# Layer 1 attention of an eight-layer kernel: the softmax's row sums from VectorE's reduction of the probabilities, or from ScalarE's accumulators

## The chip, the cores and the metric

The kernel runs on one core of one Trainium2 chip, as one program. The metric is its device time in microseconds (us), as the median of several executions.

## The reference, cut to what matters

The whole program is four pairs of a gated cross attention and a gated feed-forward layer, L0 to L3, on x of 16 batches x 128 positions x 256 features, with a context of the same shape. The part that the change touches is the attention of L1. For each batch b and each of 8 groups g it computes, with two query heads on x itself and two on the context:

```python
def _ln(x, w, b):
    mu = jnp.mean(x, axis=-1, keepdims=True)
    var = jnp.mean(jnp.square(x - mu), axis=-1, keepdims=True)
    return (x - mu) * jax.lax.rsqrt(var + EPS) * w + b
def _fp8_linear_pertensor(x, wq, w_scale, in_scale):
    xq = _div_clamp_fp8(x, in_scale)
    return jnp.einsum('bsi,oi->bso', xq * in_scale, wq) * w_scale
def _gqa(q, k, v):
    scale = 1.0 / np.sqrt(q.shape[-1])
    scores = jnp.einsum('bsghd,btgd->bghst', q, k) * scale
    p = jax.nn.softmax(scores, axis=-1)
    return jnp.einsum('bghst,btgd->bsghd', p, v)
```

Queries and keys go through `_ln` per head before `_gqa`; the heads' outputs are rounded to fp8 and projected back, and the result is added to x. The softmax needs, for every row of 128 scores, the maximum, the exponentials and their sum.

## The kernel before

A stage of the program is a list of instructions per engine; a stage starts when the signals of the one before have come. `l1_attention` first prepares weights and then runs one software pipeline over N = 128 units n = 8 b + g (16 batches x 8 groups). Everything stays on chip but the context, which is loaded once per batch. Each engine walks the same **steps** s and does in each step the work of several units, written out by hand in `tensor`, `scalar`, `vector` and `gpsimd` (lines 808 to 1040). An engine takes its instructions in that order, and a wait holds all that stands behind it. I count steps by s modulo 8 ("step 4" is s = 4, 12, 20, ...). In step s:

- TensorE: `project` of unit s-9 (L742, L745), `score` of s-12 (L754; waits for the exponentials of the unit before, s-13, since there is one bank of scores), `values` of s-14 (L763), `out_project` of s-15 (L775), `turn_heads` of s-11 (L787; waits for the norm of s-11), `turn_probs` of s-13 (L795; waits for GpSimd's scaled probabilities). In step 3 also `turn_x` (L803), the transposes of the next batch's x, which wait for ScalarE's `put_heads`.
- ScalarE: `exponent` of s-13 (L829: four activations of 128x128, one per head, each with the negated row maxima as its bias; an accumulator gives each row's sum), then the copies `put_probs` (L837) and `raw` (L846, L847), then `put_heads` of s-11 (L855, L857). In step 3 it ends with `scale_inputs` (L865, and eight activations L872) for the next batch.
- VectorE: in step 7 the sum into x (L962, L965); `quantise_out` of s-15 (L927, L899 to L906), its six instructions alternating with six `bn_stats` of s-10 (L914); in steps 4 to 7 and 0 one of the five parts of `quantise_x` for the next batch (L899, L901, L903, L905, L906 on 1024 columns; the first waits for `scale_inputs`, the last, which writes l1_xq, for the projections of the current batch); in step 3 the normalised x of the next batch (L975); then the reciprocal of the row sums of s-13 (L980), which waits for `exponent`; the norm of s-11 (six L985), which waits for GpSimd's `statistics`; and the negated maxima of s-12 (L993), which wait for `score` and for which the next step's `exponent` waits.
- GpSimd: the probabilities of s-13 times the inverse sums (L1034, waits for L980), then `statistics` of s-10, a chain of small operations on 128x6 that ends with L1026.

Names: PR is l1_pr (two buffers of 128x4x128, in fp32), rowsum is l1_rowsum (128x4 twice), pscore the bank of scores. `dve_own` is a semaphore that VectorE raises for itself where one of its instructions reads what another wrote.

Batches come once in eight steps. The five parts of `quantise_x` fall behind a `scale_inputs` whose step-3 chain runs through TensorE and ScalarE, for the batches 1 to 15 of the pipeline; the first of these (s = 12 to 16) lies in the ramp, where several of the other functions have no unit yet, and 14 follow with all of it.

Of the kernel before, what the change touches and what calls it, by code (L numbers as in the profile page):

```python
# [12 lines left out]
ALU = mybir.AluOpType  # L13
ACT = mybir.ActivationFunctionType
AXX = mybir.AxisListType.X
# [67 lines left out]
def build(nc, A, out):  # L83
    ctx = ExitStack()
    with ctx:
# [3 lines left out]
        def sb(scope, name, shape, dt=F32):  # L89
            return scope.enter_context(nc.sbuf_tensor(name, shape, dt))  # L90
# [5 lines left out]
        def begin(e, ends):  # L96
            for sem, value in ends:
                e.wait_ge(sem, value)

        dve_own = Own(ctx.enter_context(nc.semaphore("dve_own")))  # L100
# [488 lines left out]
        def l1_attention(ends, loaded, W, WX, scratch):  # L589
# [36 lines left out]
            negmax = sb(scratch, "l1_negmax", [P, 2, 4])  # L626
            rowsum = sb(scratch, "l1_rowsum", [P, 2, 4])
            PR = sb(scratch, "l1_pr", [P, 2, 4, P])
# [195 lines left out]
            def exponent(e, n):  # L824
                e.wait_ge(*s_max(n + 1))
                if n >= 2:
                    e.wait_ge(*s_ptr(n - 1))
                for h in range(4):
                    r = e.activation(PR[:, n % 2, h, :], pscore[:, h * P:(h + 1) * P], ACT.Exp,  # L829
                                     bias=negmax[:, n % 2, h:h + 1], accum_out=rowsum[:, n % 2, h:h + 1])  # L830
                r.then_inc(s_exp.sem, 1)

            def put_probs(e, n):
# [42 lines left out]
            def scalar(e):  # L876
                begin(e, ends)
                for s in range(G + N + 8):
                    if 0 <= s - 13 < N:
                        exponent(e, s - 13)  # L880
                    if s % G == 0 and 0 <= s // G - 1 < B:
                        b = s // G - 1
                        e.wait_ge(*s_ctx(b + 1))
                        if b >= 1:
                            e.wait_ge(*s_proj(G * b))
                        e.copy(tok(CX[:, :, :]), tok(CN[:, :, :])).then_inc(s_cx.sem, 1)
                    if 0 <= s - 14 < N:
                        put_probs(e, s - 14)
                    if 0 <= s - 9 < N:
                        raw(e, s - 9)  # L890
                    if 0 <= s - 11 < N:
                        put_heads(e, s - 11)
                    if s % G == 3 and s // G < B:
                        scale_inputs(e, s // G)
# [23 lines left out]
            def quantise_out(e, n):  # L918

                own = None  # L920
                for part in range(6):
                    if 0 <= n < N:
                        if part == 0:
                            e.wait_ge(*s_pv(n + 1))
                            if n >= 1:
                                e.wait_ge(*s_cat(n))
                            e.tensor_tensor(YO[:, :].rearrange("p (h t) -> p h t", h=4),  # L927
                                            pout[:, :].rearrange("p (h t) -> p h t", h=4),
                                            bc(smooth[:, n % G, :], 2, P), ALU.mult).then_inc(s_smooth.sem, 1)
                        else:  # L930
                            e.wait_ge(*(s_smooth(n + 1) if part == 1 else own))
                            if part == 5 and n >= 2:
                                e.wait_ge(*s_outp(n - 1))
                            r = round_fp8(e, part - 1, YO[:, :], EO[:, :], TO[:, :], tok(CAT[:, n % 2, :, :]))
                            if part == 5:
                                r.then_inc(s_cat.sem, 1)
                            else:
                                dve_own.did(r)
                                own = dve_own.all()
                    count(e, n + 5, part)  # L940
# [3 lines left out]
            def quantise_x(e, b, part):  # L944
                e.wait_ge(*(quantised[b] if part else s_affine(b + 1)))
                if part == 4 and b >= 1:
                    e.wait_ge(*s_proj(G * b))
                r = round_fp8(e, part, YQ[:, :], EQ[:, :], TQ[:, :], XQ[:, :, :, :].rearrange("p n k t -> p (n k t)"))
                if part == 4:
                    r.then_inc(s_xq.sem, 1)  # L950
                else:
                    dve_own.did(r)
                    quantised[b] = dve_own.all()

            def vector(e):
                begin(e, ends)
                for s in range(G + N + 9):
                    n = s - 16
                    if 0 <= n < N and n % G == G - 1:
                        b = n // G  # L960
                        e.wait_ge(*s_outp(n + 1))
                        e.scalar_tensor_tensor(X[:, b, :], pacc[:, 0:D], coef[:, 0:1], X[:, b, :],  # L962
                                               ALU.mult, ALU.add).then_inc(s_xadd.sem, 1)
                        e.wait_ge(*s_xadd(b + 1))
                        e.bn_stats(stats[:, b, :], X[:, b, :]).then_inc(bn.sem, 1)  # L965
                    quantise_out(e, s - 15)
                    if s % G >= 4 and s // G < B:
                        quantise_x(e, s // G, s % G - 4)
                    if s % G == 0 and 1 <= s // G <= B:
                        quantise_x(e, s // G - 1, 4)  # L970
                    if s % G == 3 and s // G < B:
                        b = s // G
                        if b >= 1:
                            e.wait_ge(*s_xtr(b))
                        e.tensor_scalar(xn[:, :], X[:, b, :], mean[:, b:b + 1], rstd[:, b:b + 1],  # L975
                                        ALU.subtract, ALU.mult).then_inc(s_xn.sem, 1)
                    n = s - 13
                    if 0 <= n < N:
                        e.wait_ge(*s_exp(n + 1))
                        e.reciprocal(rowsum[:, n % 2, :], rowsum[:, n % 2, :]).then_inc(s_inv.sem, 1)  # L980
                    n = s - 11
                    if 0 <= n < N:
                        e.wait_ge(*s_rstd(n + 1))
                        for m in range(6):
                            r = e.tensor_scalar(RAW[:, n % 4, m, :], RAW[:, n % 4, m, :], tiny[:, n % 2, 0, m:m + 1],  # L985
                                                tiny[:, n % 2, 6, m:m + 1], ALU.subtract, ALU.mult)
                        r.then_inc(s_norm.sem, 1)
                    n = s - 12
                    if 0 <= n < N:
                        e.wait_ge(*s_score(n + 1))  # L990
                        if n >= 2:
                            e.wait_ge(*s_exp(n - 1))
                        e.tensor_reduce(negmax[:, n % 2, :], pscore[:, :].rearrange("p (h t) -> p h t", h=4),  # L993
                                        AXX, ALU.max, negate=True).then_inc(s_max.sem, 1)
# [33 lines left out]
            def gpsimd(e):  # L1028
                begin(e, ends)
                for s in range(G + N + 8):  # L1030
# [5 lines left out]
                    if 0 <= s - 10 < N:  # L1036
                        statistics(e, s - 10)

            stage(sync=sync, tensor=tensor, scalar=scalar, vector=vector, gpsimd=gpsimd)
            return [bn(B), s_outp(N), s_pte(N), s_prob(N), s_cx(B), s_rstd(N)]  # L1040

# [1004 lines left out]
```

## Time and profile before

| | |
|---|---|
| median of 3 runs | 2855.9 us (2855.89 to 2860.24) |
| the profiled execution's own time | 2857.04 us |
| its span in the profile | 2855.2 us |
| busy, share of the span | PE 86%, PE's weight loads 72%, DVE 71%, ACT 45%, POOL 41% |
| granted TensorE clock, mean | 0.931 |

PE is TensorE, DVE VectorE, ACT ScalarE, POOL GpSimd. The attention of L1 takes some 1000 us of the span, from about 640 to 1645 us. A busy engine of a whole program says little about one stage, so the views of the stage are read for the change: the busy time in a stretch, the instructions in order of time on one engine, and the waits.

### The profile page before, as it was taken

How to read it: one execution, taken by the hardware profiler on the slowest of the kernel's cores; microseconds unless marked ns; L12 is line 12 of the kernel's file. 1: busy time of each engine (PE TensorE's matmuls, PEld its weight loads, DVE VectorE, ACT ScalarE, POOL GpSimd, SP SyncE). 2: the span in 40 equal slices, each digit the busy share in tenths (PEclk: the TensorE clock that was granted, in tenths of full speed). 3: DMA queues.
4: the chain of work that ended last, by engine and by line, in shares of the span. 5: the costliest groups of instructions: out<-in, count | busy, mean ns of one | idle time of the engine just before them, and what ended most of it. 6: DMA issues, size and time to landing. Idle time of an engine off the chain costs nothing. (4 is left out here: it accounts for less than half of the span.)

```text
span 2855.2 us, 51398 instructions
## 1 busy us (share of the span) xinstructions
PE 2451.8 (86%) x17090; PEld 2057.1 (72%) x17090; DVE 2037.1 (71%) x5105; ACT 1296.4 (45%) x3941; POOL 1179.1 (41%) x2615
## 2 busy tenths in 40 slices
PE   5758999939999999999999869999699997466997
PEld 2346777728888888888888858888588886234775
DVE  7964555558888888888888847777554554895776
ACT  0013333236666666666666623333144443344663
POOL 4401000037777777777777711111143443122112
PEclk9768999969999999999999969999799999676998
DMA  2030000010000000000000030000100000001000
GB/s 73 17 133 24 16 16 8 1 63 3 3 3 5 3 3 3 3 3 3 3 5 1 1 106 23 23 23 12 52 7 9 7 5 1 0 1 53 21 24 31
DMA packets 29155, 56.72 MB, mean 20 GB/s; under 512 B 4846, under 2 KB 22574, under 8 KB 27422
## 3 DMA queue, kind: packets, MB, share of 16 engines
q1 hardware_dynamic: 28894, 53.43, 5.7%
q8 instruction: 140, 2.29, 0.3%
q14 instruction: 121, 0.99, 0.1%
HBM read 51.33 MB, written 2.10 MB: 19 GB/s over the span
## 5 line engine op out<-in xcount | busy, mean ns | idle before, releaser
L434 PE MATMUL bank<-m_xr,m_wgr 128*88 128x512 f32 (+1 forms) x1824 | 442.3, 395 | 17.4 <-POOL m_wgr L494 17.4
L434 PEld LDWEIGHTS bank<-m_xr,m_wgr 128*88 128x88 f32 (+1 forms) x1824 | 307.3, 172 | 116.9 <-issue 19.5
L742 PE MATMUL bank<-l_w,l_xq 128*128 128x128 f32 (+1 forms) x2048 | 358.5, 328 | 9.9 <-DVE l_xq L906 7.1
L742 PEld LDWEIGHTS bank<-l_w,l_xq 128*128 128x128 f32 x2048 | 300.4, 192 | 31.1 <-DVE l_xq L906 7.5
L985 DVE TENSOR_SCALAR xn_T<-xn_T,l_tiny 128x128 f32<-128x128 f32 x768 | 297.2, 453 | 8.4 <-POOL l_tiny L1026 8.4
L494 POOL TENSOR_TENSOR m_wgr<-m_wg,m_wgr 128x512 fp32r<-128x512 f32 (+1 forms) x28 | 40.3, 1440 | 585.5 <-ACT m_wgr L472 585.5
L855 ACT ACTIVATE l_qt<-bank,l_head_b,l_head_w 128x256 f32<-128x256 f32 x256 | 144.6, 565 | 287.5 <-PE bank L787 287.5
L447 PEld LDWEIGHTS bank<-m_wdr,m_hbr 88*128 88x128 f32 (+1 forms) x1824 | 233.1, 192 | 26.9 <-DVE m_hbr L549 18.0
L447 PE MATMUL bank<-m_wdr,m_hbr 88*128 88x256 f32 (+1 forms) x1824 | 239.5, 285 | 10.1 <-DVE m_hbr L549 10.0
L582 DVE SCALAR_TENSOR_TENSOR x_resident<-bank,m_cg,x_resident 128x256 f32<-128x256 f32 x448 | 185.9, 478 | 85.4 <-PE bank L447 79.4
L484 ACT ACTIVATE m_sg<-bank 88x512 f32<-88x512 f32 (+1 forms) x152 | 90.8, 597 | 323.0 <-PE bank L434 323.0
L914 DVE BATCH_NORM_STATS2 l_st<-xn_T 128x6 f32<-128x128 f32 x768 | 214.3, 282 | 12.7 <-ACT l_v L847 12.5
L572 DVE TENSOR_TENSOR m_ht<-m_sg,bank 88x512 f32<-88x512 f32 (+1 forms) x152 | 104.3, 686 | 146.8 <-ACT m_sg L484 146.5
L1034 POOL TENSOR_TENSOR l_pr<-l_pr,l_rowsum 128x512 f32<-128x512 f32 x128 | 134.3, 1050 | 156.9 <-DVE l_rowsum L980 156.9
L829 ACT ACTIVATE l_pr<-bank,l_negmax 128x128 f32<-128x128 f32 x512 | 182.4, 385 | 1.6 <-DVE l_negmax L993 1.6
L1016 POOL TENSOR_TENSOR l_tiny<-l_tiny,l_consts 128x6 f32<-128x6 f32 x128 | 177.6, 1387 | 10.0
L775 PE MATMUL bank<-l_wp,l_cat 128*128 128x256 f32 x1024 | 167.1, 306 | 2.0 <-DVE l_cat L906 2.0
L754 PEld LDWEIGHTS bank<-l_qt 128*128 128x128 f32 x1024 | 133.8, 192 | 45.4 <-issue 39.7
L754 PE MATMUL bank<-l_qt 128*128 128x128 f32 x1024 | 137.2, 277 | 33.5 <-ACT l_pr L829 33.5
L1322 POOL TENSOR_TENSOR l_pr<-l_pr,l_rowsum 128x512 f32<-128x512 f32 x64 | 66.6, 1041 | 206.1 <-DVE l_rowsum L1289 206.1
L846 ACT COPY xn_T<-bank 128x384 f32<-128x384 f32 x256 | 125.7, 491 | 46.8 <-PE bank L745 46.8
L775 PEld LDWEIGHTS bank<-l_wp,l_cat 128*128 128x128 f32 x1024 | 140.4, 190 | 9.0 <-DVE l_cat L906 2.4
(272 smaller groups left out, 5715.2 us busy)
## 6 DMA issues: line engine op xcount, KB each, us to landing
l_w<-in_l_w SPq DMA_DIRECT2D x1, 6144.0 KB, 17.3
m_wg<-in_m_gu SPq DMA_DIRECT2D x18, 256.0 KB, 2.6
m_wg<-in_m_gu SPq DMA_DIRECT2D x10, 352.0 KB, 2.9
l2f_w<-in_l_w SPq DMA_DIRECT2D x3, 1024.0 KB, 7.5
m_wd<-in_m_down SPq DMA_DIRECT2D x18, 128.0 KB
x_resident<-in_x SPq DMA_DIRECT2D x4, 512.0 KB, 5.6
l_ctxT<-in_ctxT SPq DMA_DIRECT2D x1, 2048.0 KB, 7.1
l_toep<-in_l_toep SPq DMA_DIRECT2D x16, 128.0 KB, 2.0
```

Source lines behind the costliest of these rows:

```text
L434: r = e.matmul(banks[2 * (q % 2) + half][0:M, :], WGR[:, u % 2, a, k, sub, half, :], XR[:, b, k, cols], start=k == 0 and n == 0, stop=k == ...
L447: r = e.matmul(banks[4 + 2 * (n % 2) + s // 2][:, (s % 2) * D:(s % 2 + 1) * D], HBR[0:M, n % 2, a, sub, s * P:(s + 1) * P], WDR[0:M, u % 2 ...
L582: r = e.scalar_tensor_tensor(X[:, b, :], banks[4 + 2 * (n % 2) + s // 2][:, (s % 2) * D:(s % 2 + 1) * D], CG[:, u, b:b + 1], X[:, b, :], A ...
L742: e.matmul(bank[:, to:to + width], XQ[:, v, k, :], W[:, k, g, at:at + width], start=k == 0, stop=k == KT - 1)
L754: r = e.matmul(pscore[:, h * P:(h + 1) * P], QT[:, n % 2, x + h % 2, :], QT[:, n % 2, x + 2, :], start=True, stop=True)
L775: r = e.matmul(pacc[:, 0:D], CAT[:, n % 2, h, :], WP[:, part, head, :], start=g == 0 and h == 0 and part == 0, stop=g == G - 1 and h == 3 ...
L829: r = e.activation(PR[:, n % 2, h, :], pscore[:, h * P:(h + 1) * P], ACT.Exp, bias=negmax[:, n % 2, h:h + 1], accum_out=rowsum[:, n % 2, h ...
L855: e.activation(tok(QT[:, n % 2, 3 * x:3 * x + 2, :]), ps[:, 0:2 * P], ACT.Identity, bias=head_b[:, 2 * x:2 * x + 1], scale=head_w[:, 2 * x ...
L914: r = e.bn_stats(st[:, n % 2, m, :], RAW[:, n % 4, m, :])
L985: r = e.tensor_scalar(RAW[:, n % 4, m, :], RAW[:, n % 4, m, :], tiny[:, n % 2, 0, m:m + 1], tiny[:, n % 2, 6, m:m + 1], ALU.subtract, ALU. ...
L1016: pool_own.did(e.tensor_tensor(r0, var, minus_half, ALU.pow))
L1034: e.tensor_tensor(PR[:, n % 2, :, :], PR[:, n % 2, :, :], bc(rowsum[:, n % 2, :], 2, P), ALU.mult).then_inc(s_prob.sem, 1)
```

## The change

The four activations of `exponent` no longer have an accumulator. VectorE adds up the probabilities of the unit with one `tensor_reduce` of 128x512 to 128x4, behind the wait for the exponentials, waits for it by its own semaphore, and takes the reciprocal as before. The numbers that reach GpSimd are the same sums of the same exponentials.

```diff
                 for h in range(4):
                     r = e.activation(PR[:, n % 2, h, :], pscore[:, h * P:(h + 1) * P], ACT.Exp,
-                                     bias=negmax[:, n % 2, h:h + 1], accum_out=rowsum[:, n % 2, h:h + 1])
+                                     bias=negmax[:, n % 2, h:h + 1])
                 r.then_inc(s_exp.sem, 1)
...
                     n = s - 13
                     if 0 <= n < N:
                         e.wait_ge(*s_exp(n + 1))
+                        dve_own.did(e.tensor_reduce(rowsum[:, n % 2, :], PR[:, n % 2, :, :], AXX, ALU.add))
+                        e.wait_ge(*dve_own.all())
                         e.reciprocal(rowsum[:, n % 2, :], rowsum[:, n % 2, :]).then_inc(s_inv.sem, 1)
```

## Rows read from the trace of the kernel before

**Rows 1.** Busy time by engine in a stretch (count of instructions), granted clock, DMA share, GB/s.
```profile
640.00:1640.00 1000.00, 933.40 (x6293) 864.27 (x6292) 858.18 (x2630) 660.50 (x2295) 769.39 (x2127) 1.00 0.01 3
```

**Rows 2.** TensorE in order of time: start, us, line, operation, [idle before, released by].
```profile
1017.63 1.13 PE L754 MATMUL bank<-l_qt 128*128 128x128 f32 x8 [1.69 <-ACT l_pr L829]
...
1020.42 0.82 PE L787 MATMUL bank<-ident,xn_T 128*128 128x128 f32 x6
...
1042.41 0.88 PE L787 MATMUL bank<-ident,xn_T 128*128 128x128 f32 x6
...
1050.92 0.88 PE L787 MATMUL bank<-ident,xn_T 128*128 128x128 f32 x6 [0.60 <-DVE xn_T L985]
...
1058.27 0.82 PE L787 MATMUL bank<-ident,xn_T 128*128 128x128 f32 x6
...
1065.56 0.82 PE L787 MATMUL bank<-ident,xn_T 128*128 128x128 f32 x6
```

**Rows 3.** VectorE in order of time, steps 4 to 2 of the same batch.
```profile
1016.13 0.43 DVE L899 TENSOR_SCALAR l_yq<-l_yq 128x1024 bf16<-128x1024 bf16 x1 [3.76 <-ACT l_yq L872]
1017.52 0.18 DVE L980 RECIPROCAL l_rowsum<-l_rowsum 128x4 f32<-128x4 f32 x1 [0.96 <-ACT l_pr L829]
1017.61 2.33 DVE L985 TENSOR_SCALAR xn_T<-xn_T,l_tiny 128x128 f32<-128x128 f32 x6
...
1023.77 0.40 DVE L901 TENSOR_SCALAR l_eq<-l_yq 128x1024 uint16<-128x1024 uint16 x1
...
1024.82 2.36 DVE L985 TENSOR_SCALAR xn_T<-xn_T,l_tiny 128x128 f32<-128x128 f32 x6 [0.21 <-POOL l_tiny L1026]
...
1031.81 2.32 DVE L985 TENSOR_SCALAR xn_T<-xn_T,l_tiny 128x128 f32<-128x128 f32 x6
...
1035.19 0.48 DVE L962 SCALAR_TENSOR_TENSOR x_resident<-bank,l_coef,x_resident 128x256 f32<-128x256 f32 x1 [0.46 <-PE bank L775]
1035.71 0.43 DVE L965 BATCH_NORM_STATS2 ln_stats<-x_resident 128x6 f32<-128x256 f32 x1
...
1039.35 0.68 DVE L905 TENSOR_TENSOR l_tq<-l_yq,l_eq 128x1024 bf16<-128x1024 bf16 x1
1039.94 0.17 DVE L980 RECIPROCAL l_rowsum<-l_rowsum 128x4 f32<-128x4 f32 x1
...
1047.32 1.23 DVE L906 TENSOR_TENSOR l_xq<-l_tq,l_eq 128x1024 f32<-128x1024 bf16 x1 [1.05 <-PE bank L745]
...
1048.55 2.32 DVE L985 TENSOR_SCALAR xn_T<-xn_T,l_tiny 128x128 f32<-128x128 f32 x6
...
1055.50 2.36 DVE L985 TENSOR_SCALAR xn_T<-xn_T,l_tiny 128x128 f32<-128x128 f32 x6 [0.33 <-POOL l_tiny L1026]
...
1062.27 0.18 DVE L980 RECIPROCAL l_rowsum<-l_rowsum 128x4 f32<-128x4 f32 x1 [0.51 <-ACT l_pr L829]
```

**Rows 4.** ScalarE in order of time, the exponentials of step 4.
```profile
1016.00 0.36 ACT L829 ACTIVATE l_pr<-bank,l_negmax 128x128 f32<-128x128 f32 x1
1016.25 0.20 ACT L829 ACTIVATION_READ_ACCUMULATOR l_pr<-bank,l_negmax 128x1 f32 x1
...
1017.28 0.21 ACT L829 ACTIVATION_READ_ACCUMULATOR l_pr<-bank,l_negmax 128x1 f32 x1
```

**Rows 5.** ScalarE in order of time, exponentials of L3's attention, which have no accumulator.
```profile
2700.16 1.61 ACT L1709 ACTIVATE l_pr<-bank,l_negmax 128x256 f32<-128x256 f32 x4
2701.59 1.14 ACT L1720 COPY l_pt<-bank 128x512 f32<-128x512 f32 x2
```

**Rows 6.** VectorE's groups by form: count, busy us, mean ns, idle before.
```profile
L993 DVE TENSOR_REDUCE l_negmax<-bank 128x4 f32<-128x512 f32 x128 | 86.8, 678 | 1.1 <-PE bank L754 1.1
...
L322 DVE TENSOR_REDUCE l_sums<-l_z 128x64 f32<-128x512 f32 x64 | 66.9, 1066 | 0.0
...
L1513 DVE TENSOR_REDUCE l2f_sc<-l2f_xr 128x1 f32<-128x256 f32 x16 | 6.7, 420 | 0.6
```

**Rows 7.** Waits in the stage: who waited for whom, total us, times, longest.
```profile
PE bank L754 <- ACT l_pr L829: 33.5, 18, 2.9
```

## The prediction

> **What bounds the kernel now.** I read the stage's busy times first, then TensorE in order of time over one batch, then VectorE over the same batch, then ScalarE at the one place where TensorE waits for it. From 640 to 1640 us TensorE is busy 93% of the time and VectorE 86%, at the full granted clock of 1.00, its 2.4 GHz level [rows 1]: two engines are close to the bound, so the question is where the second becomes the first. An ordinary step lasts 1065.56 - 1058.27 = 7.29 us, without a wait on TensorE [rows 2]; there VectorE sits idle 0.51 us before its reciprocal, behind a wait for GpSimd of 0.33 [rows 3]. Such steps are TensorE's. But in three places of each batch another wait ends last:
>
> - step 4: ScalarE's exponentials start late, behind the eight activations of `scale_inputs`, and TensorE's `score` waits 1.69 us for them [rows 2]; VectorE waits 3.76 us for `scale_inputs` and 0.96 us for the exponentials [rows 3];
> - step 7: `turn_heads` starts at 1042.41, just when the norm that began at 1040.03 is through; VectorE had no idle time before that step's reciprocal;
> - step 0: TensorE idles 0.60 us before `turn_heads` for the norm (L985) [rows 2], which stands behind the last part of `quantise_x`, itself held 1.05 us by the projections [rows 3].
>
> So from step 4 to step 0 VectorE's own sequence is already the bound in two places. Work added to it there lengthens the batch, and work added in steps 1 to 3 goes into its idle time.
>
> **What the change removes.** Per unit, four accumulator reads. The activations of a unit start 0.34 us apart and each read follows its activation by 0.25 us [rows 4]: (1017.28 - 1016.25) / 3 = 0.34. Without reads I take the next activation to start 0.25 behind the one before. Activations of L3 bear that out from the other side: four of 256 columns without accumulators take 2701.59 - 2700.16 = 1.43 us of issue, 0.36 each, for twice the columns [rows 5]. The last exponential of step 4 then ends at 1016.00 + 3 x 0.25 + 0.36 = 1017.11, against 1017.28 + 0.21 = 1017.49 now: 0.38 us earlier in every step. Bounds: none of it is saved but the last read, 0.1 us (the activations keep their 0.34), or all of 0.38; I take 0.38, since two different rows give it. By the Trainium skill (ScalarE: Activation LUTs, What ACT_TABLE_LOAD costs) back-to-back activations overlap by only about 93 ns; by that estimate the exponentials of 128 columns would follow each other by some 0.29 us and end about 0.13 later than I take. The row of step 4 shows an overlap of 0.11 (0.36 - 0.25) up to the read, so it disagrees a little, and the sum would rise by about 0.13 us per batch, 2 us in all.
>
> In ordinary steps these 0.38 us are worth nothing: ScalarE is idle behind them anyway. In step 4 `score` starts 0.38 earlier. In the drain of the pipeline, where `score` waits for the exponentials too (18 waits in all, the longest 2.9 us, some four of them in the drain [rows 7]), I credit 4 x 0.38 = 1.5 us.
>
> **What it adds.** One reduction of 128x512 per unit on VectorE, 128 in all. The reduction of the maxima has the same shape, but from PSUM, and takes 0.678 us; one from SBUF of 256 columns takes 0.420, and L322, also 512 columns from SBUF but adding elements that lie 8 apart, 1.066 [rows 6]. The new one reads neighbouring elements, as L993 and L1513 do: 0.68. Then the reciprocal has to wait for it. Independent VectorE instructions overlap by 0.09 (L905 of 0.68 us, the next 0.59 after its start), while one that waits for its forerunner starts 0.04 behind its end (L962 of 0.48 us, L965 0.52 after its start) [rows 3]. So the reduction costs 0.68 + 0.04 = **0.72 us** of VectorE's sequence before the reciprocal. Bounds: 0.59 (nothing for the wait, the overlap of a free instruction) and 1.11 (L322's duration). The Trainium skill (VectorE: DVE Perf Modes, The DRAIN you can't avoid) says that a semaphore between VectorE instructions costs nothing extra. By that rule the reciprocal would start about 0.59 behind the reduction and the total would come out near +14 us; the pair L962 and L965 speaks against it, as the dependent one pays 0.52 for a duration of 0.48.
>
> What stands behind the added wait: on VectorE the norm (L985) and the maxima (L993); on GpSimd L1034 and `statistics`; on TensorE `turn_heads` and, with much time to spare, `turn_probs`. In a step where VectorE is idle before the reciprocal, that comes 0.72 - 0.38 = 0.34 us later; `turn_heads` is not touched: in step 2 the norm ends at 1062.27 + 0.09 + 2.33 = 1064.69 and `turn_heads` starts at 1065.56 [rows 2, 3], so of 0.87 us of slack 0.53 are left.
>
> **The walk through a batch**, all times 10xx.xx of rows 3 with the new cost put in:
>
> - step 4: exponentials end 17.11, reduction at 17.15 (as the reciprocal now starts 0.03 behind them), reciprocal 17.87, norm 17.96 (now 17.61).
> - step 5: 6.16 us (1023.77 - 1017.61) to L901, 24.12; reduction 0.31 later, when its 0.40 are issued, 24.43; norm at 24.43 + 0.72 + 0.09 = 25.24 (now 24.82, when it waited 0.21 for GpSimd). GpSimd's chain from one norm to the next is 7.21 here (24.82 - 17.61): 25.17, just hidden.
> - step 6: by the same spacings, 25.24 + 6.16 + 0.31 + 0.81 = 32.52 (now 31.81).
> - step 7: L962 now starts after an idle 0.46 for TensorE, 2.9 us behind the norm without it; it starts at 35.42 (now 35.19), L905 4.16 later at 39.58, reduction 40.17, norm at 40.98 (now 40.03): **+0.95**. TensorE had no slack here: `turn_heads` moves from 42.41 to 43.36.
> - step 0: the projections, and with them L906 (47.32), move by the 0.95; behind it the reduction adds its 0.72 in full, since there was no idle time before the reciprocal: norm at 48.55 + 0.95 + 0.72 = 50.22, **+1.67**. `turn_heads` waited for the norm already and moves as much.
> - step 1: GpSimd's chain, 6.95 from norm to norm (55.50 - 48.55), gives 57.17; VectorE's own, 6.26 us from the norm to the end of the work before the reciprocal (1062.27 - 0.51 - 55.50 in the next step), less an overlap of 0.09, and 0.81, gives 57.20; again +1.67, and no more. Steps 2 and 3: TensorE's, unchanged; the norm is 0.35 later than due and has its 0.5 us.
>
> The earlier `score` of step 4 is worth nothing: `turn_heads` would be ready at 1020.04 in place of 1020.42 [rows 2], but waits for the norm, 17.96 + 2.33 + 0.05 = 20.34.
>
> **Sum.** 14 full batches x 1.67 = 23.4 us; the ramp's batch, with less on VectorE, between 0 and 1.67, taken at 0.7; the drain -1.5, and +0.3 for the last unit's later reciprocal: **+22.9 us**. The profiled execution took 2857.04 us for a span of 2855.2; it would take 2879.9. Against the median of 2855.9, 1.1 below that execution, it is 2878.8; I say 2879. A measurement of this kernel can tell about 0.2%, 5.7 us, from no change.
>
> **Rivals.**
>
> 1. *The reduction is hidden, no change.* This needs VectorE to add the numbers at twice the rate of L993. The walk counts the reduction four times up to +0.95 and five times up to +1.67, so the step 0 delay vanishes at 0.72 - 1.67 / 5 = 0.39 us. From 256 to 512 columns a reduction grows by 0.678 - 0.420 = 0.258; at twice the rate 512 columns cost what 256 do now, 0.42 + 0.04 = 0.46, 0.35 us per batch, +4 us: 2860. For it: nothing but that other VectorE operations have such rates; against it: all three reductions in rows 6 take 1 ns per column or more (0.258 us for the 256 further columns). 8%.
> 2. *Faster.* The 0.38 us that the exponentials end earlier decide step 4, and VectorE takes the reduction into its waits. The place is step 0: below 0.39 us per reduction the batch gets shorter, by 0.39 less the cost. With a cost as small as the reciprocal's 0.09 that would be 0.3 x 14 + 1.5 = 5.7 us, 2851. Against it: no reduction in the trace is under 0.39 at this size. 3%.
> 3. *VectorE bounds every step.* With L322's 1.11 the five counts add 5 x 0.39 = 1.95 to the 1.67, and an ordinary step of VectorE, 6.3 us from one reciprocal to the place of the next, grows to 7.4, over TensorE's 7.29; with step 3's extra instruction some 0.5 us more per batch. 4.1 x 14 = 58, about 2914. For it: the buffer is in SBUF, as L322's. Against it: L1513. 5%.
> 4. *ScalarE saves nothing* since activations keep 0.34: the exponentials of step 4 end 0.28 later than I take, 14 x 0.28 = 4 us more and no gain in the drain: 2884. 6%, still slower.
>
> The forecast's own mechanism, with the bounds of its terms, has the remaining 78%. Its own ends: 0.59 per reduction gives 1.67 - 5 x 0.13 = 1.02 per batch and +14 (2870); 0.85, if the reduction is held up by GpSimd or the wait costs more than L965's, gives +9 more (2888). The range reaches to most of the no-change case below and past rival 4 above, for stalls of TensorE that the walk doesn't see: 2863 to 2896. Faster 3% is rival 2; within 0.2% 9% is rival 1 and 1% of the forecast's low end; the rest, 88%, is slower.
>
> **What the changed profile would show.** L829's activations about 0.25 us apart and no accumulator reads; 128 new reductions at L980's place of 0.68 us, the reciprocal 0.72 behind their start; in step 0 the norm 1.67 us later within the batch, TensorE's idle before `turn_heads` grown from 0.60 to about 1.3, and in step 7 a new one of about 0.8; ordinary steps still 7.29. I am wrong if the reduction takes under 0.5 or over 0.9 us, if the ordinary steps grow, or if GpSimd's chain rather than VectorE's ends last in step 5 or 6.

## The result, and the profile after

The changed kernel takes **2879.9 us** (median of 4 runs, 2879.7 to 2885.4) against 2857.5 for the kernel before in the same comparison: a ratio of 1.0081 (95% interval 1.0068 to 1.0093). The forecast was slower, 2879 us, with a range of 2863 to 2896. The profiled execution took 2879.81 us for a span of 2878.0, 22.8 us over the span of before. Two lines are new, so the reduction is L980, the reciprocal L982, GpSimd's scaling L1036, the norm L987, the maxima L995.

Busy time of the stretch that [rows 1] shows for before:

```profile
640.00:1640.00 1000.00, 922.15 (x6187) 851.11 (x6185) 914.96 (x2702) 601.70 (x1752) 772.38 (x2095) 1.00 0.01 3
```

TensorE is down from 93.3% to 92.2%, VectorE up from 86% to 91%, ScalarE down from 66% to 60%, at the same clock. VectorE in order of time over one batch after the change, steps 4 to 2, which answers to [rows 3]:

```profile
1090.42 0.43 DVE L899 TENSOR_SCALAR l_yq<-l_yq 128x1024 bf16<-128x1024 bf16 x1 [3.39 <-ACT l_yq L872]
1091.43 0.69 DVE L980 TENSOR_REDUCE l_rowsum<-l_pr 128x4 f32<-128x512 f32 x1 [0.58 <-ACT l_pr L829]
1092.15 0.18 DVE L982 RECIPROCAL l_rowsum<-l_rowsum 128x4 f32<-128x4 f32 x1
1092.25 2.32 DVE L987 TENSOR_SCALAR xn_T<-xn_T,l_tiny 128x128 f32<-128x128 f32 x6
...
1098.72 0.67 DVE L980 TENSOR_REDUCE l_rowsum<-l_pr 128x4 f32<-128x512 f32 x1
...
1099.53 2.32 DVE L987 TENSOR_SCALAR xn_T<-xn_T,l_tiny 128x128 f32<-128x128 f32 x6
...
1106.81 2.32 DVE L987 TENSOR_SCALAR xn_T<-xn_T,l_tiny 128x128 f32<-128x128 f32 x6
1109.05 0.68 DVE L995 TENSOR_REDUCE l_negmax<-bank 128x4 f32<-128x512 f32 x1
1109.65 0.47 DVE L962 SCALAR_TENSOR_TENSOR x_resident<-bank,l_coef,x_resident 128x256 f32<-128x256 f32 x1
...
1115.19 2.32 DVE L987 TENSOR_SCALAR xn_T<-xn_T,l_tiny 128x128 f32<-128x128 f32 x6
...
1122.48 1.22 DVE L906 TENSOR_TENSOR l_xq<-l_tq,l_eq 128x1024 f32<-128x1024 bf16 x1 [1.05 <-PE bank L745]
1123.62 0.68 DVE L980 TENSOR_REDUCE l_rowsum<-l_pr 128x4 f32<-128x512 f32 x1
1124.33 0.18 DVE L982 RECIPROCAL l_rowsum<-l_rowsum 128x4 f32<-128x4 f32 x1
1124.42 2.33 DVE L987 TENSOR_SCALAR xn_T<-xn_T,l_tiny 128x128 f32<-128x128 f32 x6
...
1131.38 2.35 DVE L987 TENSOR_SCALAR xn_T<-xn_T,l_tiny 128x128 f32<-128x128 f32 x6
```

Between the wait for the exponentials of step 4 (0.58) and that for the projections in step 0 (1.05) the view shows no idle time of VectorE. The norms start 7.28, 7.28, 8.38 and 9.23 us apart; before it was 7.21, 6.99, 8.22 and 8.52. TensorE, which answers to [rows 2], in the same batch:

```profile
1091.54 1.13 PE L754 MATMUL bank<-l_qt 128*128 128x128 f32 x8 [1.30 <-ACT l_pr L829]
1094.62 0.88 PE L787 MATMUL bank<-ident,xn_T 128*128 128x128 f32 x6
...
1117.57 0.88 PE L787 MATMUL bank<-ident,xn_T 128*128 128x128 f32 x6 [0.87 <-DVE xn_T L987]
...
1126.81 0.87 PE L787 MATMUL bank<-ident,xn_T 128*128 128x128 f32 x6 [1.33 <-DVE xn_T L987]
...
1134.15 0.82 PE L787 MATMUL bank<-ident,xn_T 128*128 128x128 f32 x6
```

`score` in step 4 waits 1.30 in place of 1.69; step 7 has a wait of 0.87 that was not there; that of step 0 has grown from 0.60 to 1.33; the ordinary step behind it takes 7.34 us from one `turn_heads` to the next, the one after that 7.29. ScalarE in step 4 of that batch, and VectorE's two reductions by form, which answer to [rows 4] and [rows 6]:

```profile
1090.30 1.10 ACT L829 ACTIVATE l_pr<-bank,l_negmax 128x128 f32<-128x128 f32 x4
```

```profile
L980 DVE TENSOR_REDUCE l_rowsum<-l_pr 128x4 f32<-128x512 f32 x128 | 86.7, 678 | 18.1 <-ACT l_pr L829 17.9
L995 DVE TENSOR_REDUCE l_negmax<-bank 128x4 f32<-128x512 f32 x128 | 86.6, 676 | 0.9 <-PE bank L754 0.9
```

Four exponentials take 1.10 us from the first start to the last end (I took 3 x 0.25 + 0.36 = 1.11), and the reduction 0.678 (I took 0.68).

**Where the 22.8 us lie.** I read the start of the first `project` instruction (L742) of a unit in both traces. The first are those of unit 8, the second those of unit 120, before:

```profile
671.03 2.79 PE L742 MATMUL bank<-l_w,l_xq 128*128 128x256 f32 x16
...
1560.26 2.79 PE L742 MATMUL bank<-l_w,l_xq 128*128 128x256 f32 x16
```

and after:

```profile
672.22 2.79 PE L742 MATMUL bank<-l_w,l_xq 128*128 128x256 f32 x16
...
1583.51 2.79 PE L742 MATMUL bank<-l_w,l_xq 128*128 128x256 f32 x16
```

Fourteen batches take 889.2 us before, 63.52 each, and 911.3 after, 65.09 each: **+22.1 us**, 1.58 per batch. Unit 0 starts at 614.63 before and 613.43 after, 1.20 earlier (that is ahead of the changed part, and differs as much between executions of other kernels below); counted from there, the ramp up to unit 8 adds 2.39. From the last unit's `project` on, the drain gives back 0.9. -1.2 + 2.4 + 22.1 + 0.3 (the seven steps from unit 120 to 127) - 0.9 = 22.7.

### The profile page after: what moved, and what is told of

Its sections match the earlier page's. It is cut to its first block and busy times, and to the rows that moved or that the text cites. A ratio compares the mean times of both kernels' runs of the same rounds, so it can differ in the third digit from the quotient of the medians.

```text
span 2878.0 us, 51014 instructions
## 1 busy us (share of the span) xinstructions
PE 2455.1 (85%) x17090; PEld 2059.8 (72%) x17090; DVE 2115.0 (73%) x5233; ACT 1248.7 (43%) x3429; POOL 1193.9 (41%) x2615
## 5 line engine op out<-in xcount | busy, mean ns | idle before, releaser
L742 PE MATMUL bank<-l_w,l_xq 128*128 128x128 f32 (+1 forms) x2048 | 360.2, 329 | 9.9 <-DVE l_xq L906 7.1
L742 PEld LDWEIGHTS bank<-l_w,l_xq 128*128 128x128 f32 x2048 | 301.8, 193 | 31.4 <-DVE l_xq L906 7.5
L987 DVE TENSOR_SCALAR xn_T<-xn_T,l_tiny 128x128 f32<-128x128 f32 x768 | 296.2, 452 | 0.0
L1036 POOL TENSOR_TENSOR l_pr<-l_pr,l_rowsum 128x512 f32<-128x512 f32 x128 | 135.2, 1056 | 166.0 <-DVE l_rowsum L982 166.0
L829 ACT ACTIVATE l_pr<-bank,l_negmax 128x128 f32<-128x128 f32 x512 | 147.1, 387 | 1.6 <-DVE l_negmax L995 1.6
L549 DVE TENSOR_TENSOR m_hbr<-m_ht,m_hbr 88x512 fp32r<-88x512 f32 (+1 forms) x152 | 125.6, 826 | 28.9 <-ACT m_hbr L488 28.9
```

The lines of the kernel that those rows point to most:

```text
L742: e.matmul(bank[:, to:to + width], XQ[:, v, k, :], W[:, k, g, at:at + width], start=k == 0, stop=k == KT - 1)
L1036: e.tensor_tensor(PR[:, n % 2, :, :], PR[:, n % 2, :, :], bc(rowsum[:, n % 2, :], 2, P), ALU.mult).then_inc(s_prob.sem, 1)
```

## The experiments

The theory was that of the forecast: VectorE's order from the exponentials of step 4 to the norm of step 0 sets the length of a batch, the reduction costs it 0.72 us at a time, and what ScalarE saves counts once, 0.38 us in step 4. The rivals: that the saving is worth nothing; that VectorE's total work counts, wherever it stands; that the waits of TensorE have other causes. "Per batch" below is read as above, from unit 8 to unit 120 over 14; the kernel before had medians of 2857.0 to 2858.8 us in these comparisons.

| kernel | median us | ratio to before, 95% | per batch us |
|---|---|---|---|
| before | 2857.0 to 2858.8 | | 63.52 |
| changed | 2879.9 | 1.0068 to 1.0093 | 65.09 |
| e1, accumulators and reduction | 2890.1 | 1.0097 to 1.0128 | 65.48 |
| e2, neither | 2850.7 | 0.9963 to 0.9985 | 63.13 |
| e3, two reductions | 2952.7 | 1.0319 to 1.0347 | 69.74 |
| e4, sums first in step 0 | 2871.4 | 1.0033 to 1.0058 | 64.39 |
| e5, change in steps 1 to 3 | 2857.1 | 0.9992 to 1.0011 | 63.48 |
| e6, change in steps 4 to 0 | 2884.5 | 1.0080 to 1.0107 | 65.10 |
| e7, norm ahead, accumulators | 2845.0 | 0.9939 to 0.9964 | 62.67 |
| e8, norm ahead, changed | 2850.7 | 0.9964 to 0.9982 | 63.15 |
| e9, change in step 4 | 2859.6 | 0.9998 to 1.0016 | 63.47 |
| e10, norm ahead, change in step 4 | 2839.2 | 0.9923 to 0.9948 | 62.32 |
| e11, as e7 | 2842.1 | 0.9939 to 0.9966 | 62.67 |
| e12, GpSimd's scaling cut | 2852.0 | 0.9964 to 0.9982 | 63.11 |

**e1: accumulators and reduction.**

```diff
-                                     bias=negmax[:, n % 2, h:h + 1])
+                                     bias=negmax[:, n % 2, h:h + 1], accum_out=rowsum2[:, n % 2, h:h + 1])
```

> The changed kernel with the accumulators back, written to a tile that nobody reads; the reduction stays. Theory (VectorE's sequence from the exponentials of step 4 to the norm of step 0 sets the batch; the reduction costs it five times, the reads' removal gives back 0.38 us once, in step 4): the exponentials of step 4 end 0.38 us later and the whole chain with them, 15 x 0.38 and 4 x 0.38 in the drain, about +7 us on the changed kernel, 2887 us. Rival (taking the reads away was worth nothing, and what was measured is the reduction alone): as the changed kernel, 2880.

2890.1 us, +0.39 us per batch on the changed kernel, and `score` waits 1.68 again. The median is 3 us over the forecast, the profiled execution is at 2887.9. Of the batch only step 4 is longer, from one `project` to the next 9.56 us in place of 9.18: the reads are worth 0.38 there, where VectorE's chain starts behind them, and nothing in the other steps.

**e2: neither.** The row sums are left out.

```diff
-                        dve_own.did(e.tensor_reduce(rowsum[:, n % 2, :], PR[:, n % 2, :, :], AXX, ALU.add))
-                        e.wait_ge(*dve_own.all())
-                        e.reciprocal(rowsum[:, n % 2, :], rowsum[:, n % 2, :]).then_inc(s_inv.sem, 1)
+                        e.reciprocal(rowsum[:, n % 2, :], ones4[:, :]).then_inc(s_inv.sem, 1)
```

> The kernel before without the accumulators and without any sum: the reciprocal is taken of a constant tile, so the probabilities are scaled by a constant and the row sums are left out. Theory: 0.38 us per batch in step 4 and four times in the drain, 7 us under the kernel before, 2850 us. Rival (the earlier score is lost again at the next wait, by step 7 at the latest): same as the kernel before, 2857.

2850.7 us, 0.39 per batch under the kernel before. So the change has two parts that add up: the saving, -0.39, and the reduction, 65.09 - 63.13 = +1.96 per batch; with the accumulators kept (e1 against the kernel before) it is 65.48 - 63.52 = 1.96 too.

**e3: a second reduction** into a tile that nobody reads, ahead of the first.

```diff
+                        dve_own.did(e.tensor_reduce(rowsum2[:, n % 2, :], PR[:, n % 2, :, :], AXX, ALU.add))
                         dve_own.did(e.tensor_reduce(rowsum[:, n % 2, :], PR[:, n % 2, :, :], AXX, ALU.add))
```

> The changed kernel with a second reduction of the same probabilities into a tile that nobody reads, ahead of the first, so VectorE has 0.59 us more per unit. Theory: five times 0.59 = 2.95 us per batch in steps 4 to 0, and now VectorE's ordinary step (6.26 + 0.59 + 0.81 - 0.09 = 7.57) is over TensorE's 7.29, so steps 1 to 3 add 0.28, 0.28 and 0.59 less the 0.5 of slack: about 3.6 us per batch, 14 x 3.6 = 50, about 2930 us (2920 to 2945), and idle time of TensorE before turn_heads in every step. Rival (each reduction costs what the first did, 23 us, with ordinary steps still TensorE's): 2903.

2952.7 us, beyond the 2945 that I had allowed: 4.65 per batch on the changed kernel in place of 3.6. The linear rival is out, and so is my sum. TensorE in step 0 and its granted clock around it (the second fence: stretch, length, busy, clock, DMA share, GB/s):

```profile
1090.10 0.88 PE L788 MATMUL bank<-ident,xn_T 128*128 128x128 f32 x6 [1.92 <-DVE xn_T L989]
...
1091.45 4.24 PE L743 MATMUL bank<-l_w,l_xq 128*128 128x256 f32 x16
```

```profile
1088.00:1090.00 2.00, 0.19 (x2) 1.00 0.00 0
1090.00:1092.00 2.00, 1.90 (x12) 0.76 0.04 8
1092.00:1094.00 2.00, 2.00 (x8) 0.50 0.00 0
1094.00:1096.00 2.00, 2.00 (x13) 0.89 0.01 4
```

With one reduction TensorE idled 1.33 us there at most; now it idles 1.92, and in this batch its clock falls from the 2.4 to the 1.2 GHz level behind that. The 16 instructions take 4.24 us in place of 2.79. The wait alone does not decide it: of the fourteen waits of 1.85 to 1.92 us in step 0 of the full batches six are followed by such a fall and eight are not, and two more falls come behind waits of 1.47 us for `put_heads` in step 3. The four batches that no fall touches take 69.13 or 69.14 us, 4.04 over the changed kernel, and the average is 69.74, so the falls are 8.6 of the 15 us that my sum missed. The other 6 lie in step 3, which grew by 0.57 us where I had put 0.09: with VectorE the bound in steps 1 and 2 already, the slack that I subtracted was gone, and TensorE waits 0.36 us for the norm there. The norms are 7.88 and 7.87 apart in steps 5 and 6, the 0.59 more that the theory gave.

**e4: sums first in step 0**, reduction and reciprocal moved ahead of the last part of `quantise_x`. `inverse` holds the wait for the exponentials, the reduction, its wait and the reciprocal.

```diff
+                    early = s % G == 0
+                    if early:
+                        inverse(s - 13)
...
                     if s % G == 0 and 1 <= s // G <= B:
                         quantise_x(e, s // G - 1, 4)
```

> The changed kernel, but in step 0 VectorE takes reduction and reciprocal ahead of the last part of quantise_x, into the 1.06 us that it idles there for the projections. Theory (in step 0 the reduction stands in full between the projections' end and the norm that TensorE waits for): the norm of step 0 starts 0.81 us earlier, 14 x 0.81 = 11 us under the changed kernel, 2869 us; TensorE's idle before turn_heads in step 0 falls from 1.32 to about 0.5. Rival (TensorE's wait there is set by the last part of quantise_x or by GpSimd's chain, not by the reduction): 2880.

2871.4 us; TensorE's wait in step 0 falls from 1.33 to 0.60, and a batch is shorter by 0.70 of the 0.81 us. Here a second thing shows, VectorE and GpSimd in order of time:

```profile
1055.02 1.94 DVE L906 TENSOR_TENSOR l_xq<-l_tq,l_eq 128x1024 f32<-128x1024 bf16 x1 [0.26 <-PE bank L745]
1056.88 1.68 DVE L978 TENSOR_SCALAR xn_T<-xn_T,l_tiny 128x128 f32<-128x128 f32 x6
```

```profile
1054.84 1.04 POOL L1044 TENSOR_TENSOR l_pr<-l_pr,l_rowsum 128x512 f32<-128x512 f32 x1 [0.19 <-DVE l_rowsum L972]
```

The instruction that now runs beside GpSimd's scaling takes 1.94 us in place of 1.22, and the norm, which runs beside it in all other steps, 1.68 in place of 2.32. The difference of the two, 0.08, is most of what is missing from the 0.81. That led to e12.

**e5 and e6: one half of the steps each.** The condition picks units by their step; the others keep the accumulators. e5 has steps 1, 2, 3 and e6 steps 4, 5, 6, 7, 0.

```diff
+                    more = {} if (n + 13) % G in (1, 2, 3) else dict(accum_out=rowsum[:, n % 2, h:h + 1])
...
+                        if (n + 13) % G in (1, 2, 3):
                             dve_own.did(e.tensor_reduce(rowsum[:, n % 2, :], PR[:, n % 2, :, :], AXX, ALU.add))
```

> The change in steps 1, 2 and 3 alone (48 of 128 units); in steps 4 to 0 the accumulators stay. Theory (in those steps the reduction lies in idle time of VectorE): same as the kernel before, 0 to +2 us, about 2858. Rival (what counts is VectorE's total work, wherever it stands): three eighths of 23 us, +9, 2867.

> The other half: the change in steps 4, 5, 6, 7 and 0 alone (80 of 128 units), accumulators in steps 1 to 3. Theory: all of the changed kernel's loss, +22 us, 2880. Rival (total work counts): five eighths, +14, 2872.

Per batch 63.48 and 65.10: three eighths of the reductions cost nothing, the other five eighths all of it. The rival of total work is out. e6 as a whole is 4 us over its forecast. That is not in the batches. Counted from unit 0 its last unit starts 25.0 us later than before (24.8 in the changed kernel), and the first transposes of the next stage 27.7 (23.9): the 3.6 us lie in the drain. The units whose exponentials TensorE waits for there keep their accumulators, and the three waits are 2.86 us in place of the changed kernel's 2.50, 1.1 in all, which my forecast had left out; and the clock is 0.68 from 1650 to 1660 us, where the changed kernel has 1.00.

```profile
1650.00:1660.00 10.00, 7.14 (x33) 6.55 (x32) 5.79 (x15) 3.58 (x13) 4.27 (x9) 0.68 0.01 2
```

**e7 and e8: the norm ahead** on the kernel before and on the changed one. In step 4 the norm stands ahead of the first part of `quantise_x` and its wait of 3.76 us, in step 0 reciprocal and norm ahead of the last part.

```diff
+                    if s % G == 0:
+                        inverse(s - 13)
+                    if s % G in (0, 4):
+                        norm(s - 11)
                     if s % G >= 4 and s // G < B:
                         quantise_x(e, s // G, s % G - 4)
...
+                    if s % G != 0:
+                        inverse(s - 13)
+                    if s % G not in (0, 4):
+                        norm(s - 11)
```

> The kernel before, with VectorE's order changed in two of eight steps: in step 4 the norm (L985) stands ahead of the first part of quantise_x and its wait, in step 0 reciprocal and norm ahead of the last part. Accumulators as before. Theory (in step 0 TensorE waits for VectorE's order, 1.2 us per batch: the step takes 8.51 against 7.29): the norm of step 0 starts when GpSimd's chain allows, 6.95 behind that of step 7, 1.6 us earlier, and TensorE no longer waits; 14 x 1.2 = 17 us, 2841. Rival (the last part of quantise_x, now 2.3 us later, holds the projections of the next batch, or GpSimd is the next bound): no gain, 2858 or more.

> The same reordering on the changed kernel. Theory (the reduction costs what VectorE's order lets through to the norms that TensorE waits for; with the norm ahead in steps 4 and 0 two of the five counts vanish, steps 5, 6, 7 still hand on some 0.7, and step 1 about 0.5): the changed kernel's loss is mostly gone, but not below the same order with accumulators: 2852 to 2862, 2857. Rival (VectorE's total work is the bound once the reduction is in): stays near 2880.

`turn_heads` of step 0 in e7, and of step 7 in e8:

```profile
1106.77 0.82 PE L787 MATMUL bank<-ident,xn_T 128*128 128x128 f32 x6
```

```profile
1103.46 0.87 PE L787 MATMUL bank<-ident,xn_T 128*128 128x128 f32 x6 [0.69 <-DVE xn_T L978]
```

e7: 2845.0 us, 0.85 per batch in place of 1.2. From one `project` to the next step 0 takes 7.69 us in place of 8.51: the wait of 0.60 for the norm is gone, and some 0.2 us more around it. The rest of step 0's length is `values`, which comes 1.20 behind `score` there in place of 0.89, and which I had counted as the norm's: it waits for ScalarE's `put_probs` (L837), and that stands behind a copy (L886) that waits 0.86 us for the projections. e8: 2850.7, below the kernel before and 29 us below the changed one, better than forecast. With the norm of step 4 out of the way the earlier `score` counts: from one `project` to the next, step 4 falls from 9.18 to 8.82, and step 0 from 9.23 to 7.70. The same change then costs 63.15 - 62.67 = 0.48 us per batch in place of 1.58: against e7 step 7 is 0.72 longer, where `turn_heads` waits 0.69 for the norm, step 1 is 0.12 longer, and step 4 is 0.37 shorter. The reduction's price is one of place.

**e9, e10, e11.** The change in step 4 alone (`(n + 13) % G == 4`), without and with the norm ahead; e11 is e7's kernel again beside e10.

> The change in step 4 alone (16 of 128 units), nothing moved. Theory: score starts 0.38 us earlier, but turn_heads waits for the norm of step 4, 0.34 later than before; VectorE's extra 0.34 is taken up by its waits of steps 5 and 6, so nothing reaches step 7: same as the kernel before, within 1 us. Rival (each of the five reductions costs its fifth of the 22 us): +4.4.

> The kernel before with the norm ahead in steps 4 and 0 (as in the run of that order with accumulators), and the change in step 4 alone. Theory (with the norm out of the way the earlier exponentials of step 4 reach TensorE, and one reduction there fits VectorE's waits): 0.38 us per batch under the same order with accumulators, 15 x 0.38 = 5.7 us, in all 12 + 6 = 18 to 19 us under the kernel before, about 2839. Rival (the 0.34 us of the later reciprocal come out at GpSimd's chain and the norm of step 5): as the same order with accumulators, 2845.

> The same kernel as the one with the norm ahead and all accumulators, beside the one above on the same chip for their difference: 12 to 13 us under the kernel before, 5 to 6 above the one with the change in step 4. Rival: no difference between the two.

e9 is the kernel before within the measurement (63.47 per batch): one reduction is taken up by the waits of steps 5 and 6. e10 is **2839.2 us, 0.64% under the kernel before** and 1.4% under the changed one, the fastest here. Its 62.32 per batch are 0.35 below e11's (forecast 0.38), and its waits show why: in the full batches `score` waits 1.30 in place of 1.67, and `turn_heads` for no norm.

```profile
1071.74 1.13 PE L754 MATMUL bank<-l_qt 128*128 128x128 f32 x8 [1.30 <-ACT l_pr L830]
1074.52 0.82 PE L787 MATMUL bank<-ident,xn_T 128*128 128x128 f32 x6
```

In medians the two are 2.9 us apart and their intervals overlap; that e10 is the faster of the two rests on the batches.

**e12: GpSimd's scaling cut** to 8 of each 128 columns, on the changed kernel. The rest of the probabilities stay unscaled.

```diff
-                        e.tensor_tensor(PR[:, n % 2, :, :], PR[:, n % 2, :, :], bc(rowsum[:, n % 2, :], 2, P),
+                        e.tensor_tensor(PR[:, n % 2, :, 0:8], PR[:, n % 2, :, 0:8], bc(rowsum[:, n % 2, :], 2, 8),
```

> The changed kernel with GpSimd scaling only 8 of each 128 columns of the probabilities (the rest of that scaling is left out), so that L1036 takes some 0.2 us in place of 1.05. In the traces the norm, six instructions at L985, takes 2.32 us wherever that GpSimd instruction runs beside it, and 1.62 to 1.68 in the places where it doesn't (steps whose order was changed). Theory (the two hold each other up over SBUF, and 0.65 us of VectorE's step are that): the norm falls to about 1.65 in every step; in step 7 TensorE's wait is gone but for 0.1 to 0.2, in step 0 it is 0.65 shorter; 65.1 us per batch fall to 63.4 to 63.7, 20 to 24 us under the changed kernel, about 2858. Rival (the norm's length is its own, and GpSimd only shortens its own chain): norm at 2.32, time as the changed kernel, 2880.

2852.0 us, some 6 below its forecast. VectorE in step 0, and GpSimd's group:

```profile
1044.92 1.23 DVE L906 TENSOR_TENSOR l_xq<-l_tq,l_eq 128x1024 f32<-128x1024 bf16 x1 [1.06 <-PE bank L745]
1046.07 0.68 DVE L980 TENSOR_REDUCE l_rowsum<-l_pr 128x4 f32<-128x512 f32 x1
1046.87 1.60 DVE L987 TENSOR_SCALAR xn_T<-xn_T,l_tiny 128x128 f32<-128x128 f32 x6
```

```profile
L1036 POOL TENSOR_TENSOR l_pr<-l_pr,l_rowsum 128x32 f32<-128x32 f32 x128 | 32.6, 254 | 248.9 <-DVE l_rowsum L982 248.9
```

The norm takes 1.60 us in every step of the full batches but step 1, where it takes 1.63. The batch takes 63.11, less than before the change, with the reduction in it; the forecast had left out that the earlier `score` of step 4 counts again once the norm is not late (that step takes 8.82 in place of 9.18). GpSimd's own chain is shorter too in e12, so the time alone would not show the cause; the norm's length does. In the changed kernel all that the norm loses falls on one of its six instructions, the one that starts while the scaling runs; the other five take 0.32 to 0.34 us (first VectorE in step 7, then GpSimd):

```profile
1115.43 1.06 DVE L987 TENSOR_SCALAR xn_T<-xn_T,l_tiny 128x128 f32<-128x128 f32 x1
```

```profile
1115.36 1.05 POOL L1036 TENSOR_TENSOR l_pr<-l_pr,l_rowsum 128x512 f32<-128x512 f32 x1 [0.83 <-DVE l_rowsum L982]
```

The Trainium skill (SBUF — State Buffer, Practical consequences) says that a VectorE instruction in a mode that uses two ports and a GpSimd instruction exclude each other at SBUF for a whole instruction, and that `tensor_reduce` never contends. That the norm runs in such a mode no run shows, but by that rule the trace agrees: its one instruction ends just behind the scaling, and the norm loses 0.72 us beside a GpSimd instruction of 1.05. No reduction of the probabilities runs beside the scaling in the changed kernel, so its 0.678 us say nothing on that; the maxima of step 4 do in e8, 14 times in full, and take 0.69 us in place of 0.68.

## Why the prediction was right

Point by point, by its own steps.

- *Which places bound the batch.* Right, shown by e5, e6 and e9: steps 1 to 3 free, steps 4 to 0 all of the cost, one reduction alone free. The cost is not a fifth for each; the idle time of steps 5 and 6 is used up first.
- *What is removed.* 0.38 us earlier exponentials, measured 0.39 per batch in e1 and in e2. The activations start 0.25 us apart, as I took, so the estimate of 0.29 between them, with its 2 us more in all, is out. On the changed kernel `score` starts 0.39 earlier and `turn_heads` of step 4 does not profit, as said.
- *What is added.* 0.72: the reciprocal starts 0.72 and 0.71 behind the reduction (1091.43 to 1092.15, 1123.62 to 1124.33). That independent ones overlap is shown by e3, where the second reduction starts 0.60 behind the first, and by the kernel before, where the reciprocal starts 0.59 behind an L905 of 0.68 us. So the rule of the Trainium skill (VectorE: DVE Perf Modes, The DRAIN you can't avoid) that a semaphore between VectorE instructions costs nothing extra, with the +14 us that I worked out by it, does not hold here: the wait costs 0.12 us.
- *The walk.* Forecast spacings of the norms in steps 5 to 0: 7.28, 7.28, 8.46, 9.24; measured 7.28, 7.28, 8.38, 9.23. The one that is off is step 7: I took 2.9 us from the norm to L962 without its wait, which was the end of the maxima; it is 2.84 (1106.81 to 1109.65), since they overlap. 1.67 per batch became 1.58, 23.4 us became 22.1.
- *The ramp.* Forecast 0.7, measured 2.4. This term was mis-sized. TensorE waited 1.95 us for a norm there (1.23 before), and the 16 instructions behind it took 4.44 us in place of 2.79 at a granted clock of 0.50: up to 1.65 us that the walk of VectorE does not contain. The rest, some 0.7, is what I had put. A wait of 2.34 us in the same ramp, for `put_heads`, left the clock at 1.00.

```profile
632.07 0.41 PE L803 MATMUL bank<-ident,l_xn 128*128 128x128 f32 x2 [2.34 <-ACT l_qt L857]
...
646.49 0.87 PE L787 MATMUL bank<-ident,xn_T 128*128 128x128 f32 x6 [1.95 <-DVE xn_T L987]
```

```profile
648.00:650.00 2.00, 2.00 (x8) 0.50 0.00 0
```

- *The drain.* Forecast -1.2, measured -0.9, and that they are close is luck too. I had counted some four waits for the exponentials; both traces have three, 2.86 us before and 2.50 after. Up to the last `out_project` the drain is only 0.25 us shorter, since behind the third wait it takes 0.7 us more where I had put 0.3. The other 0.64 us are that `out_project` itself, at a granted clock of 0.50 before and 1.00 after. Its rows before and after:

```profile
1648.62 1.86 PE L775 MATMUL bank<-l_wp,l_cat 128*128 128x256 f32 x8 [2.01 <-DVE l_cat L906]
```

```profile
1671.93 1.22 PE L775 MATMUL bank<-l_wp,l_cat 128*128 128x256 f32 x8 [2.00 <-DVE l_cat L906]
```

- *The total.* +22.9 forecast for the span, +22.8 measured. That they agree to 0.1 us is luck: the ramp's +1.7, step 7's -1.3, the +0.3 of the last seven steps, the drain's +0.3 and a start of the stage that lay 1.2 us earlier cancel. In the stage itself it is +23.9.
- *Rivals.* That L322's 1.07 us would be the price is out (0.678). I had no experiment on why L322 is slower; that it adds elements 8 apart is the one difference that I name, not shown as its cause.

## What to carry to other kernels

An accumulator that rides on another engine's instruction cost little here (0.39 us per batch of some 64); summing in an instruction of its own was dear or free by its place in the busy engine's order. So walk one period of that order with its waits: find between which two waits the engine never rests, and count the new instruction once for each pass through that part. Before weighing which engine should do a piece of work, look at what stands ahead of the instruction that TensorE waits for; moving the norm ahead of a wait in two of eight steps gained more here (0.5%) than leaving the sum out altogether (0.3%), and only then did a reduction in step 4, with its earlier exponentials, pay (e9 against e10).

## What the runs showed of the hardware that I had not expected

- VectorE's norm (six instructions of 128x128 in fp32, SBUF to SBUF) takes 2.32 us while GpSimd's scaling of 1.05 us runs, 1.60 when that is cut to 0.25 (e12). One of the six takes 1.06 us in place of 0.34. In the kernel before this lies in 126 of the 128 units.
- TensorE's granted clock fell to 0.50, the 1.2 GHz level, behind a wait of 1.95 us in the changed kernel's ramp and, in e3, behind six waits of 1.9 and two of 1.47 us, in a stretch where it was busy 89% of the time. The length of one wait does not tell: eight other waits of 1.9 us in e3, one of 2.34 in the ramp and those of 1.33 in step 0 left it at 1.00. In e3 a batch with such a fall inside took up to 70.5 us, one without 69.1.
- Four exponentials of 128 columns without accumulators follow each other at 0.25 us, with accumulator reads at 0.34: the read itself is recorded with 0.23 us but costs 0.09 of issue.
